# Second layer's attention on one Trainium2 core: the row maxima subtracted by VectorE on the way out of PSUM, the finished values copied out by ScalarE

## The reference, cut to what matters

```python
q_full = jnp.concatenate([q_abs, q_pe], axis=-1)          # 16 heads, 64 + 64 wide
k_full = jnp.concatenate([ckv, k_pe[:, :, 0, :]], axis=-1)  # the same keys for all heads
sm_scale = (DN + DR) ** (-0.5)
scores = jnp.einsum('bqhd,bkd->bhqk', q_full, k_full) * sm_scale
scores = jnp.where(causal[None, None], scores, jnp.finfo(scores.dtype).min)
attn = jax.nn.softmax(scores, axis=-1)
o_ckv = jnp.einsum('bhqk,bkr->bqhr', attn, ckv)
y = jnp.einsum('bqhr,hre->bqe', o_ckv, w_o_abs)
```

## Time and profile before

| | |
|---|---|
| median of 3 runs | 2325.57 us |
| profiled execution, its time | 2323.5 us |
| its span | 2322.0 us |
| mean granted TensorE clock | 0.919 |
| TensorE busy | 2008.8 us (87%) |
| VectorE busy | 1449.2 us (62%) |
| ScalarE busy | 1252.5 us (54%) |
| GpSimd busy | 876.0 us (38%) |

### The profile page before, as it was taken

One profiled execution on the slowest core, in us unless ns is written; L12 is line 12 of the kernel. 1 busy time (PEld: TensorE's weight loads), 2 busy tenths in 40 slices (PEclk: granted clock), 3 DMA queues, 4 the chain that ended last, 5 costly groups with the idle time before them and its releaser, 6 DMA issues. The chain is left out here.

```text
span 2322.0 us, 41383 instructions
## 1 busy us (share of the span) xinstructions
PE 2008.8 (87%) x11710; PEld 1336.4 (58%) x11710; DVE 1449.2 (62%) x3073; ACT 1252.5 (54%) x2550; POOL 876.0 (38%) x899
## 2 busy tenths in 40 slices
PE   4886999999767769999738899999788999997698
PEld 1442233333144559999714577777544777775587
DVE  4776888888055669999447665665255555543443
ACT  0573577777733337777214477777144777771322
POOL 1221000000035547798153177777100666670100
PEclk7895799999977879999869999999898999998899
DMA  7953000000061148899421011212000011112000
GB/s 212 289 95 46 11 1 0 0 0 1 25 183 78 69 138 262 264 281 278 139 68 50 8 44 42 50 44 53 19 0 1 24 23 32 23 35 68 0 19 18
DMA packets 186850, 173.82 MB, mean 75 GB/s; under 512 B 20755, under 2 KB 171653, under 8 KB 185734
## 3 DMA queue, kind: packets, MB, share of 16 engines
q1 hardware_dynamic: 174662, 143.23, 22.3%
q0 software_dynamic: 10720, 29.44, 3.8%
q10 hardware_dynamic: 1376, 0.02, 0.0%
HBM read 96.15 MB, written 61.60 MB: 68 GB/s over the span
## 5 line engine op out<-in xcount | busy, mean ns | idle before, releaser
L2611 POOL TENSOR_TENSOR w_rest<-work,w_head 128x512 fp32r<-128x512 f32 (+3 forms) x384 | 395.3, 1042 | 223.5 <-ACT w_head L2568 221.1
L769 DVE TENSOR_REDUCE half_max<-m_ps 128x1 f32<-128x512 f32 x512 | 316.6, 682 | 53.7 <-PE m_ps L694 53.2
L2457 DVE TENSOR_REDUCE piece_max<-m_ps 128x1 f32<-128x512 f32 (+3 forms) x384 | 200.8, 548 | 203.4 <-PE m_ps L2384 159.9
L823 ACT ACTIVATE weights<-s_ps 128x512 f32<-128x512 f32 x512 | 266.4, 602 | 100.1 <-PE s_ps L709 100.1
L2564 ACT ACTIVATE work<-s_ps 128x512 f32<-128x512 f32 (+3 forms) x384 | 187.6, 488 | 100.9 <-PE s_ps L2412 96.0
L2568 ACT ACTIVATE w_head<-work 128x512 fp32r<-128x512 f32 (+3 forms) x384 | 201.4, 524 | 57.0 <-PE o_ps L2421 46.0
L694 PE MATMUL m_ps<-kT,qT 96*128 (+1 forms) x512 | 211.8, 416 | 6.5 <-DVE half_max L769 4.5
L709 PE MATMUL s_ps<-qT,kT 99*128 (+1 forms) x512 | 191.3, 386 | 7.3 <-ACT weights L823 7.3
L2421 PE MATMUL o_ps<-w_head,lat_head 128*128 128x512 f32 (+3 forms) x384 | 184.3, 480 | 1.6 <-POOL w_rest L2611 1.5
L859 POOL COPY v_now<-v 128x83 f32 (+1 forms) x64 | 16.1, 258 | 375.3 <-PE o_ps L721 370.0
L709 PEld LDWEIGHTS s_ps<-qT,kT 99*128 (+1 forms) x512 | 49.0, 98 | 160.7 <-ACT weights L823 66.8
(11 more groups left out here) (393 smaller groups left out, 5038.6 us busy)
## 6 DMA issues: line engine op xcount, KB each, us to landing
slots<-zero SPq DMA_DIRECT2D x8, 3456.0 KB, 27.4
rows<-slots SPq DMA_DIRECT2D x64, 256.0 KB, 3.4
slots<-ex_out SPq DMA_DIRECT2D x64, 256.0 KB, 3.0
ex_wgv<-in_L_ffn_wg_dram SPq DMA_DIRECT2D x72, 176.0 KB, 3.0
ex_wgv<-in_L_ffn_wv_dram SPq DMA_DIRECT2D x72, 176.0 KB, 3.2
ex_wo<-in_L_ffn_wo_dram SPq DMA_DIRECT2D x72, 128.0 KB, 3.1
oT<-work SPq DMA_DIRECT2D x64, 128.0 KB
w_down<-l_inverse SPq DMA_DIRECT2D x32, 256.0 KB
```

The lines of the kernel that those rows point to most:

```text
L769: dve.tensor_reduce(half_max[:, u:u + 1], m_ps[:, BANK[u], :], AX.X, ALU.max).then_inc(max_done, 1)
L823: act.activation(w[:, s % 2 * 4 + j, :], s_ps[:, BANK[4 * s + j], :], ACT.Exp, scale=HD ** -0.5).then_inc(w_done, 1)
L2457: dve.tensor_reduce(piece_max[:, qt, k0 // 512:k0 // 512 + 1], m_ps[:, r % 2, 0:n], AX.X, ALU.max).then_inc(d["max_done"], 1)
L2611: pool.tensor_tensor(w_rest[:, s % 3, c0:512], w[:, s % 3, c0:512], w_head[:, s % 3, c0:512], ALU.subtract).then_inc(d["w_rest_done"], 1)
```

## The change

The product L2412 goes. VectorE instead subtracts `shiftT` from the bank into `w` (`subtract`), and ScalarE's exponential works in place on `w`. A new semaphore `s_read` counts the subtractions; TensorE waits on it before it reuses a bank, and ScalarE before its exponential. VectorE's order is now by tile: the subtraction of a tile first, then the maxima and other work that `AHEAD` gives to that tile. The copy of finished values moves from VectorE to ScalarE, after the rounded copies of tile 4 (previous head, second half) and tile 8 (this head, first half). ScalarE's first pair is written out ahead of the loop.

```diff
                 def scores(h, u_h, s, ahead):
-                    pe.wait_ge(d["w_done"], (h + h0) * NC + (FREE_S + s - 2))
+                    pe.wait_ge(d["s_read"], (h + h0) * NC + (FREE_S + s - 2))
+                    diagonal = kt >= 4 * qh
...
-                    if s == 0:
-                        pe.wait_ge(d["sh_copied"], h + (h0 + 1))
-                    pe.matmul(s_ps[:, u, c0:512], c.shift_rows[:, :], shiftT[:, u_h, q0:qh * 512 + 512],
-                              start=False, stop=True).then_inc(d["s_done"], 1)
...
+                def subtract(h, u, s):
+
+                    qh, kt, c0 = COLS[s]
+                    n = (h + h0) * NC + s
+                    dve.wait_ge(d["s_done"], n + 1)
+                    dve.wait_ge(d["w_rest_done"], n + (FREE_R - 2))
+                    if s == 0:
+                        dve.wait_ge(d["sh_copied"], h + (h0 + 1))
+                    dve.tensor_tensor(w[:, s % 3, c0:512], s_ps[:, s % 3, c0:512],
+                                      shiftT[:, u, qh * 512 + c0:qh * 512 + 512], ALU.subtract).then_inc(d["s_read"], 1)
...
+                    for s in range(NC):
+                        subtract(h, u, s)
+                        for r in AHEAD.get(s, ()):
+                            if ahead:
+                                maximum(h + 1, r)
+                            if later is not None and r == 2 and behind:
+                                combine(pair if u else pair - 1, 2 if u else TOPK - 1)
+                            if later is not None and r in (6, 10):
+                                combine(pair, 3 * u + (r - 6) // 4)
+                            if behind and r == 1:
+                                query_rest(h, 1)
+                            if u == 1 and r == 5 and not (isinstance(pair, int) and pair == 0):
+                                normalise(pair - 1)
+                            if u == 0 and r == 9 and behind:
+                                invert(pair - 1)
...
                 def weights(h, s):
-                    act.wait_ge(d["s_done"], (h + h0) * NC + (s + 1))
-                    act.wait_ge(d["w_rest_done"], (h + h0) * NC + (FREE_R + s - 2))
-                    act.activation(w[:, s % 3, c0:512], s_ps[:, s % 3, c0:512], ACT.Exp, scale=SM1
+                    act.wait_ge(d["s_read"], (h + h0) * NC + (FREE_S + s + 1))
+                    act.activation(w[:, s % 3, c0:512], w[:, s % 3, c0:512], ACT.Exp, scale=SM1
...
                         weights(h, s)
+                        if behind and s == 4:
+                            evacuate(h - 1, 1)
                         if ahead and s == 6:
                             query_head(h + 1, 0)
+                        if s == 8:
+                            evacuate(h, 0)
```

More of the change, by code:

```diff
@@ L2403, in scores @@
                     for i, (ks, qs) in enumerate(((k_head, q_head), (k_head, q_rest), (k_rest, q_head))):
-                        pe.matmul(s_ps[:, u, c0:512], ks[:, keys], qs[:, qh, c0:512], start=i == 0, stop=False)
+                        x = pe.matmul(s_ps[:, u, c0:512], ks[:, keys], qs[:, qh, c0:512], start=i == 0,
+                                      stop=i == 2 and not diagonal)
+                    if not diagonal:
+                        x.then_inc(d["s_done"], 1)
                     if ahead:
@@ L2407, in scores @@
                             row_scores(h + 1, r)
-                    if kt >= 4 * qh:
-                        pe.matmul(s_ps[:, u, c0:c0 + P], c.identb[:, :], c.mask_kq[:, :], start=False, stop=False)
-                    if s == 0:
-                        pe.wait_ge(d["sh_copied"], h + (h0 + 1))
-                    pe.matmul(s_ps[:, u, c0:512], c.shift_rows[:, :], shiftT[:, u_h, q0:qh * 512 + 512],
-                              start=False, stop=True).then_inc(d["s_done"], 1)
+                    if diagonal:
+                        pe.matmul(s_ps[:, u, c0:c0 + P], c.identb[:, :], c.mask_kq[:, :], start=False, stop=True
+                                  ).then_inc(d["s_done"], 1)
                 def outputs(h, s):
@@ L2506, in head @@
                 def head(h, u, pair, ahead, behind=True):
[L2508 to L2526, removed]
@@ L2527, in head @@
-                    if ahead:
-                        join(h + 1)
+                    for s in range(NC):
[13 more added lines that the diff above has]
+                                invert(pair - 1)
+                            if ahead and r == 10:
+                                query_rest(h + 1, 0)
+                            if ahead and r == NR - 1:
+                                join(h + 1)
@@ L2530, in _ @@
                 if b == 0:
                     dve.sem_inc(d["max_done"], FREE_M)
-                    dve.sem_inc(d["o_read"], FREE_O)
+                    dve.sem_inc(d["s_read"], FREE_S)
                 dve.memset(piece_max[:, 0:4, 1], -3e38).then_inc(d["preset"], 1)
@@ L2551, in _ @@
                 head(H1 - 1, 1, HP - 1, False)
-                evacuate(H1 - 1, 1)
                 if later is not None:
@@ L2575, in query_head, with evacuate @@
                                    ).then_inc(d["q_head_done"], 1)
+                def evacuate(h, qh):
+                    n = h + h0
+                    act.wait_ge(d["pv_done"], n * NC + (FREE_W + LAST[qh] + 1))
+                    if not (isinstance(h, int) and n == 0):
+                        act.wait_ge(d[f"moved{qh}"], n * 32)
+                    act.activation(staged[:, qh, :], o_ps[:, qh, :], ACT.Copy).then_inc(d["o_read"], 1)
                 def place_shift(h, u):
@@ L2580, in place_shift, with head @@
                                    ).then_inc(d["sh_copied"], 1)
-                def head(h, u, ahead):
+                def head(h, u, ahead, behind=True):
                     for s in range(NC):
@@ L2592, in _ @@
                 if b == 0:
-                    act.sem_inc(d["w_done"], FREE_S)
+                    act.sem_inc(d["o_read"], FREE_O)
                 for n in range(2):
@@ L2598, in _ @@
                 place_shift(0, 0)
-                with act.Fori(0, HP - 1) as pair:
+                head(0, 0, True, behind=False)
+                head(1, 1, True)
+                with act.Fori(1, HP - 1) as pair:
                     head(pair * 2, 0, True)
@@ L2603, in _ @@
                 head(H1 - 1, 1, False)
+                evacuate(H1 - 1, 1)
             @block.gpsimd
@@ L2690, in layer1_attention @@
                  "at_done at_copied q_done q_abs q_mul q_rot turned qT_done v_done ones_done max_done m_done parts_done "
-                 "shT_done sh_copied w_done s_done pv_done o_read inv2_done sums_loaded moved0 moved1 inv_stored inv_loaded scaled preset y_done y_added one_done "
+                 "shT_done sh_copied w_done s_done s_read pv_done o_read inv2_done sums_loaded moved0 moved1 inv_stored inv_loaded scaled preset y_done y_added one_done "
                  "got0 got1 got2 got3 got4 late0 late1 late2 added stats_done aggr_done x_eps_done x_std_done rstd_done vh_done k_head_done k_rest_done q_head_done q_rest_done w_head_done w_rest_done")
```

3 lines of the change are left out of this document (1 added, 2 removed).

## The result

The changed kernel took 2368.57 us (median of four runs, 2362.14 to 2372.88), the kernel before 2328.57 us in the same comparison. The ratio is 1.0174, 95% interval 1.0132 to 1.0217: 1.7% slower. The forecast was 2365. (Before has one run more here than the three of 2325.57 above.)

What follows compares the result with a forecast made beforehand. TensorE was taken to bound both attention stages. Second element +13 us, first +30, first pairs and last chains about +3 make 46 on 2323.5, 2369; less 4 for overlapping waits, 2365, range 2322 to 2400.

Steps and rivals of the forecast that it cites:

- 63 us: TensorE, both attention stages: removing 384 matmuls with the row of maxima saves 1.98 us a head, 63.4 us over 32 heads.
- the 16.9 that I had for TensorE alone: TensorE in the second element: its own work would need 16.9 us a head after the change.
- rival (c): VectorE's subtraction contends with GpSimd and costs 1.37 us at 512 columns, total 2430 us; chance 0.07.
- The walk, second element: One second-element head followed engine by engine: even heads 21.2 us, odd 18.5, a pair 39.7 against 37.83.
- the 0.55 us for the multiplication of oT: Odd second-element heads: this 1.63 us step precedes tile 4's subtraction, so row 8 of the next head waits about 0.55.
- in each loop turn's even head, a table load: ScalarE before tile 0's exponential: a 1283 ns load delays its start from 2.35 to 3.6 us in even heads.
- The reciprocal's wait: VectorE in even heads: waits 2.5 us for the sums after ScalarE's later copy; some 2.3 us reach the head's end.
- Rival (a): Waits largely hide in one another, leaving queueing of 0 to 0.6 us a head: say 2335 us; chance 0.20.
- The first element: Attention of the first batch element: even heads 22.9 us, odd 21.3, a pair 44.2 against 39.9, +30 us over seven.
- subtractions queue behind the same waits: VectorE, first element: subtractions stand behind combinations' waits for gathers, part of the +4.3 us a pair.
- the 4 us taken off for waits that overlap: Whole kernel: waits counted one after another can overlap, so 2369 us was lowered by 4 to 2365.

Runs made afterwards that it cites:

- x10: The changed kernel with the reciprocal behind tile 10's subtraction and the next head's row pieces spread over other tiles; ratio to the kernel before 1.003.
- x8: The changed kernel with a small square root on ScalarE that puts the table load back in its loop; ratio to the kernel before 1.0195.
- x4: The changed kernel with only the reciprocal moved, from behind maximum 9 to behind tile 10's subtraction; ratio to the kernel before 1.0095.
- x6: As x4, with a head's three row combinations moved behind the subtractions of tiles 9, 10 and 11; ratio to the kernel before 1.0108.
- x9: The changed kernel with expert rows still fetched and awaited, but not multiplied and added by VectorE; ratio to the kernel before 1.0136.
- x5: The changed kernel with expert rows of the second batch element neither fetched nor combined; ratio to the kernel before 0.9952.
- x1: The kernel before with only ScalarE's first pair written out ahead of its loop; ratio to the kernel before 0.9989.
- x11: First element keeps the product, with ScalarE copying finished values; second element as x4; ratio to the kernel before 0.993.
- x7: As x4, with the query remainder of the second half moved from behind maximum 1 to behind maximum 3; ratio to the kernel before 1.0241.

## Why the prediction was right

**The bound and the gain.** TensorE was the bound, and its 63 us were the most that could be won. No kernel here tells the price of the product apart from what replaced it; the nearest is x10's even head with 17.76 us against the 16.9 that I had for TensorE alone.

**VectorE's and ScalarE's prices.** The subtraction took 688 ns at 512 columns (x72 in the second element's window), forecast 691; rival (c) is out. The exponential from SBUF took 630 ns, forecast 632:

```profile
L2476 DVE TENSOR_TENSOR work<-s_ps,work 128x512 f32<-128x512 f32 x72 | 49.6, 688 | 28.7 <-PE s_ps L2412 21.4 <-PE s_ps L2404 6.3
...
L2563 ACT ACTIVATE work<-work 128x512 f32<-128x512 f32 x72 | 45.3, 630 | 35.4 <-DVE work L2476 35.2
```

**The walk, second element.** An odd head was 18.5 by the walk and is 18.49, but not by its parts. Tile 4 starts at 6.31 where the walk had 6.1, and the 0.55 us for the multiplication of oT did not appear: it runs in 1.22 us now, not 1.63, and the rest of the head takes 12.18 us. An even head was 21.2 and is 20.02. The step that failed is "in each loop turn's even head, a table load". The change writes ScalarE's first pair out, and the load left the loop with it; I took it from the old trace. Putting it back (x8) gives 20.5, so the load was also overpriced, 0.5 us instead of 1.0. The rest of the even head is read from x4, which has neither load nor wait: 18.42 us where the walk without both has 17.95, so 0.5 too little there and 0.7 too much for what the reciprocal passes on.

**The reciprocal's wait.** Forecast 2.5 us, measured 2.39, with the sums landing at t = 13.7 (14.6) and VectorE there at 11.4 (12.05). Of the 2.3 us that I passed on to the head's end, x4 finds 1.6 in the second element and 0.45 in the first, where my sum had 1.6. Rival (a), that waits hide in one another, holds there for this term.

**The first element.** Forecast +4.3 us a pair, measured +4.20. That the sum came out is luck. The walk had even heads of 22.9 us and odd of 21.3; they took 22.0 each. The even 22.9 hold 1.0 for the load that is not there and 1.6 for the reciprocal, of which x4 finds 0.45, so 2.1 us too much, and the rest of the pair was 2.0 too short. Queueing is the right kind of cause, but the step "subtractions queue behind the same waits" put too much on VectorE. Moving the combinations out of its way gained 0.5 (x6), leaving out their arithmetic 0.7 (x9), leaving out fetches and waits too 5.4 (x5). The trace of after shows a link that the walk did not have. A subtraction also waits until the remainder of three tiles earlier has freed its buffer of `w`, and in the first element, 1380 to 1600 us, that is VectorE's longest wait (us in all, times, longest):

```profile
DVE work L2476 <- POOL w_rest L2625: 19.9, 14, 1.9
...
DVE x L2506 <- DMA w_down<-slots,slot: 5.2, 5, 1.1
```

A fetch takes 0.96 us of GpSimd's time ahead of a remainder, three times a head. In x5, and in the second element of after, VectorE has no such wait; in x9 it is still 20.3 us. So the fetches reach VectorE through the late remainders rather than through the waits for the rows. How much of the 4.7 goes this way was not tried by itself.

**The clock** was in no term. Over the first element's attention, 1323 to 1672 us, TensorE's mean granted clock was 0.96 of full speed, against 1.00 before (1320 to 1637 us). If TensorE had bound all of that stage, 0.04 x 349 = 14 us of the first element's 34 went that way (estimate, an upper bound). No run tried the clock by itself.

**The sum.** Second element +0.68 a pair instead of +1.9 (8 pairs: +5, where seven were forecast at +13), first element +34 instead of +30, total 39 for 43. The load and the passing on were both too high, in both elements. What made up for them was the first element's missing 2.0 us a pair, the clock's share among it, and the 4 us taken off for waits that overlap. The direction and the wait at the reciprocal were understood; that the total came within 4 us of the median is in part luck.

## What to carry to other kernels

Taking work off the busiest engine is worth little where a chain of three engines already fills the cover. Here the product was priced at 3.96 us a pair, and the second element kept 0.75 of it with the reciprocal moved (x4 against x1) and 1.4 at best (x10). Add the new link to the chain and ask which wait in the same in-order queue it now stands behind. The same edit can pay in one stage and cost in another that shares its code; price the stages apart, and take each where it pays (x11). A copy of a finished value looks free to move, but what reads it next decides where it may go: here two moves and a load, 4.6 us from the start of the copy to the sums, and then a reciprocal.

## What the runs showed of the hardware

**VectorE against GpSimd.** An instruction of VectorE with both inputs in SBUF stretched from 0.68 to 3.26 us while GpSimd ran three remainders back to back (x6). The Trainium skill, SBUF — State Buffer, section Who interferes with whom, says that a VectorE instruction with two SBUF inputs contends with a GpSimd instruction that reads SBUF, and calls the shared pair of ports an exclusive lock. The row agrees, and adds that VectorE waited for more than one of GpSimd's instructions: it ended at 1466.42, 0.55 us behind the third remainder. Where such an instruction stands in VectorE's order then decides its length: 0.68, 1.54 or 1.98 us on average for the same query remainder in after, x7 and x6 (first element).

**The granted clock after a wait.** In after, TensorE waited 1.84 us at 1471.05 for a remainder. Right behind it matmuls of 512 columns end 0.42 us apart instead of 0.23. The granted clock reads 0.58 of full speed over the next 4 us, a mean of the two levels (1.2 and 2.4 GHz) and mostly the lower: from 1473 to 1475 us it is 0.50. Then it is 1.00 again:

```profile
1471.05 0.50 PE L2421 MATMUL o_ps<-w_head,lat_head 128*128 128x512 f32 x1 [1.84 <-POOL w_rest L2625]
1471.40 0.44 PE L2421 MATMUL o_ps<-w_rest,lat_head 128*128 128x512 f32 x1
1471.63 0.63 PE L2421 MATMUL o_ps<-w_head,lat_rest 128*128 128x512 f32 x1
```

```profile
1471.00:1475.05 4.05, 4.00 (x18) 3.24 (x19) 1.40 (x5) 3.96 (x9) 2.96 (x3) 0.58 0.54 138
1475.10:1479.00 3.90, 3.67 (x25) 2.69 (x24) 2.50 (x6) 2.19 (x6) 1.78 (x4) 1.00 0.10 29
```

The length of the one wait does not tell which level comes. In the same trace the clock stayed at 1.00 behind a wait of 2.03 us at 1384.23, and it was 0.61 over 4 us behind waits of 1.24 and 0.90 us at 1493.82 and 1495.75. In the second element it stayed at 1.00 behind waits of 1.4 us. That waiting brought the clock down at all was not tried by itself.
